# The mixer's inverse root-mean-squares: spread by TensorE from a repeated column instead of from VectorE's diagonal matrix

## What is computed

```python
y = (y_fw + y_bw) + xs * (xs @ fcD_w.T + D)        # "in" and "fd"
yz = y * silu(z)
y = yz * rsqrt(mean(square(yz), -1) + 1e-05) * norm_w   # "out": mean of squares; "scale"
h = y @ out_w.T
...
h = xmid + alpha * xmid + (1 - alpha) * h          # after the second turn
x = x_init + h @ w_up.T + b_up                     # "up", "rest"
```

## Time and profile before

| | before |
|---|---|
| time, median of 3 runs | 755.34 us (755.06 to 757.87) |
| span of the profiled execution | 756.9 us |
| PE busy | 713.5 us (94%) |
| DVE, ACT, POOL busy | 474.8, 318.3, 314.5 us (63%, 42%, 42%) |
| chain that ended last, by engine | PE 76%, DVE 12%, issue 5%, ACT 2%, POOL 1% |
| the mixer in the span | about 487 to 556 us |

### The profile page before, as it was taken

One profiled execution on the slowest core, in us unless ns is written; L12 is line 12 of the kernel. 1 busy time (PEld: TensorE's weight loads), 2 busy tenths in 40 slices (PEclk: granted clock), 3 DMA queues, 4 the chain that ended last, 5 costly groups with the idle time before them and its releaser, 6 DMA issues.

```text
span 756.9 us, 10266 instructions
## 1 busy us (share of the span) xinstructions
PE 713.5 (94%) x3718; PEld 431.1 (57%) x3718; DVE 474.8 (63%) x716; ACT 318.3 (42%) x536; POOL 314.5 (42%) x254
## 2 busy tenths in 40 slices
PE   4998899999999999889999999999789999999998
PEld 2444334333333332258788888554358788877886
DVE  3787677888888885237765558768895433338211
ACT  3311267677767767751335310554234223223100
POOL 0325673756565574861456233115431222125300
PEclk9999799999999999999999999999889999999999
DMA  8357516263251200230023100213010111111111
GB/s 307 107 126 220 124 43 164 73 123 54 72 123 26 30 3 29 75 113 14 29 62 105 56 1 0 78 50 66 1 68 1 57 55 39 44 55 57 42 69 42
DMA packets 24111, 53.00 MB, mean 70 GB/s; under 512 B 4252, under 2 KB 8100, under 8 KB 23044
## 3 DMA queue, kind: packets, MB, share of 16 engines
q1 hardware_dynamic: 24068, 52.44, 25.0%
HBM read 45.63 MB, written 6.60 MB: 69 GB/s over the span
## 4 chain that ended last, share of the span: by engine, by line
PE 76%; DVE 12%; issue 5%; DMA 2%; ACT 2%; SPq 2%; POOL 1%; DVEq 0%; ACTq 0%; POOLq 0%
PE ps L867 73%; DVE mxp L1810 2%; DMA rq<-in_mask 1%; DVE st L1652 1%; PE ps L884 1%; DVE xnb L1676 1%; ACT pr L1456 1%; DVE x L2007 1%; PE ps L1051 1%; DVE rt L1691 1%; DVE x L1894 1%; PE ps L1119 0%; DVE dg L2041 0%; SPq L717 0%; DVE qsw L1861 0%
## 5 line engine op out<-in xcount | busy, mean ns | idle before, releaser
L867 PE MATMUL ps<-arena 128*128 128x512 f32 (+1 forms) x1404 | 325.9, 392 | 1.4 <-DVE arena L1695 0.7
L867 PEld LDWEIGHTS ps<-arena 128*128 128x128 f32 (+1 forms) x1404 | 259.6, 186 | 59.3 <-DVE arena L1695 1.4
L1810 DVE TENSOR_REDUCE mxp<-ps 128x2 f32<-128x1024 f32 (+3 forms) x160 | 172.8, 1115 | 44.5 <-PE ps L867 43.9
L1456 ACT ACTIVATE pr<-ps 128x512 f32<-128x512 f32 x288 | 162.1, 596 | 75.7 <-PE ps L867 71.9
L867 PE MATMUL ps<-Qst,Kst 99*128 99x512 bf16 x288 | 100.2, 389 | 6.1 <-ACT pr L1456 4.8
L867 PE MATMUL ps<-Kst,Qst 96*128 96x512 bf16 (+3 forms) x384 | 98.6, 334 | 5.4 <-DVE mxp L1810 4.2
L2248 POOL TENSOR_TENSOR pr<-pr,cap 128x512 int32<-128x512 int32 x56 | 71.1, 1285 | 38.3 <-ACT pr L1456 38.3
L867 PE MATMUL ps<-pr,vr 128*32 128x512 f32 x576 | 76.5, 604 | 0.0
L867 PEld LDWEIGHTS ps<-Qst,Kst 99*128 99x128 bf16 x288 | 24.5, 98 | 79.7 <-ACT pr L1456 63.9
L867 PEld LDWEIGHTS ps<-Kst,Qst 96*128 96x128 bf16 x384 | 36.4, 99 | 51.3 <-DVE mxp L1810 20.2
L2347 POOL TENSOR_TENSOR arena<-raw,arena 128x1024 fp32r<-128x1024 f32 x11 | 26.7, 2431 | 80.2 <-ACT arena L1530 80.2
(11 more groups left out here) (203 smaller groups left out, 822.2 us busy)
## 6 DMA issues: line engine op xcount, KB each, us to landing
wmr<-in_wmr SPq DMA_DIRECT2D x8, 1280.0 KB, 11.0
raw<-in_w SPq DMA_DIRECT2D x16, 512.0 KB, 3.3
Qst<-q_parts SPq DMA_DIRECT2D x42, 128.0 KB
q_parts<-qparts SPq DMA_DIRECT2D x3, 768.0 KB, 5.0
x<-in_x SPq DMA_DIRECT2D x8, 256.0 KB, 6.0
wm<-in_wm SPq DMA_DIRECT2D x4, 512.0 KB, 7.5
raw<-in_up SPq DMA_DIRECT2D x8, 256.0 KB, 2.6
raw<-in_down SPq DMA_DIRECT2D x8, 256.0 KB, 2.6
```

What stands on the lines that cost most here:

```text
L867: return nc.tensor.matmul(outp, lhs, rhs, start=start, stop=stop, skip_group_check=True)
L1456: A(pr[:, k % PRING, :], ps[:, 4 + k % 2, :], ACT.Exp, scale=float(DH) ** -0.5).then_inc(exp_done, 1)
L1810: V.tensor_reduce(mxp[:, kh, g0:g0 + heads, i].rearrange("p (b e) -> p b e", e=per), units, AXX, ALU.max)\
```

## The change

`dg`, its four VectorE instructions and its semaphore go. In the step `scale` TensorE now issues four multiplications of 128 x 128: the stationary operand is one column of `hrs`, read 128 times with a stride of zero, the moving one the identity. Element (i, j) of the product is the sum over k of hrs[k] times identity[k, j], that is hrs[j] on every row. TensorE waits for `hrs` itself (`mr_ready`). GpSimd, before it overwrites `hrs`, now waits until the last `rbc` is written instead of for `dg`, and its `shift` no longer waits for `dg`. Apart from the removals VectorE's list has one move: `rest` of the second half comes behind `fd` and `scale` of the second turn.

```diff
-MIXER_DVE = [("fd", 0, 0), ("rows", 0, 0), ("dg", 0, 0), ("scale", 0, 0), ("fd", 0, 1), ("centred", 0, 0),
-             ("centred", 0, 1), ("dg", 0, 1), ("fd_first", 1, 0), ("scale", 0, 1), ("fd_second", 1, 0), ("rest", 0, 0), ("merge", 0, 0),
-             ("rest", 0, 1), ("dg", 1, 0), ("fd", 1, 1), ("scale", 1, 0), ("dg", 1, 1), ("up", 0, 0), ("scale", 1, 1),
+MIXER_DVE = [("fd", 0, 0), ("rows", 0, 0), ("scale", 0, 0), ("fd", 0, 1), ("centred", 0, 0),
+             ("centred", 0, 1), ("fd_first", 1, 0), ("scale", 0, 1), ("fd_second", 1, 0), ("rest", 0, 0), ("merge", 0, 0),
+             ("fd", 1, 1), ("scale", 1, 0), ("rest", 0, 1), ("up", 0, 0), ("scale", 1, 1),
              ("up", 0, 1), ("up", 1, 0), ("up", 1, 1)]
...
                 elif kind == "scale":
 
-                    pe.wait_ge(dg_ready, 2 * y + hf + 1)
+                    pe.wait_ge(mr_ready, 2 * y + hf + 1)
                     b = bank_of(pe, ("rbc", y, hf))
-                    mm(ps[:, b, :], ones[:, :], dg[:, :, :].rearrange("p t n -> p (t n)"), True, True)\
-                        .then_inc(full_b[b], 1)
+                    for t in range(4):
+                        last = mm(ps[:, b, tl(t)], hrs[:, t:t + 1].to_broadcast([P, P]), ident[:, :], True, True)
+                    last.then_inc(full_b[b], 1)
...
-                elif kind == "dg":
-                    dve.wait_ge(mr_ready, 2 * y + hf + 1)
-                    if 2 * y + hf:
-                        filled(dve, ("rbc", y if hf else 0, 1 - hf))
-                    V.tensor_tensor(dg[:, :, :], ident[:, :].unsqueeze(1).to_broadcast([P, 4, P]),
-                                    hrs[:, :].unsqueeze(2).to_broadcast([P, 4, P]), ALU.mult).then_inc(dg_ready, 1)
...
                 if kind == "out":
                     pool.wait_ge(ms_ready, 2 * y + hf + 1)
                     if 2 * y + hf:
-                        pool.wait_ge(dg_ready, 2 * y + hf)
+                        filled(pool, ("rbc", y if hf else 0, 1 - hf))
                     nc.gpsimd.tensor_tensor(hrs[:, :], hms[:, :], mh[:, :], ALU.pow).then_inc(mr_ready, 1)
                 elif kind == "shift":
-                    pool.wait_ge(dg_ready, 2)
                     for t in range(4 * hf, 4 * hf + 4):
                         rest(t)
```

More of the change, by code:

```diff
@@ L491, in adaln_two_blocks @@
         yz = at("yz", [P, 2, T], F32, ACT_B + 80 * 1024)
-        dg = at("dg", [P, 4, P], F32, HT_B + 26 * 1024)
         rb = at("rb", [P, HALF], F32, HT_B + 28 * 1024)
@@ L607, in adaln_two_blocks @@
         eps_ready, hor_ready = sem("eps_ready"), sem("hydra_out_copied")
-        ms_ready, mr_ready, dg_ready = sem("mean_squares_ready"), sem("inverse_rms_ready"), sem("inverse_rms_diagonal_ready")
+        ms_ready, mr_ready = sem("mean_squares_ready"), sem("inverse_rms_ready")
         mixw_in = sem("mixer_weights_loaded")
```

## The result

| | before | with the change |
|---|---|---|
| time, median of 10 runs | 757.85 us (755.06 to 758.74) | 752.39 us (750.0 to 755.11) |
| ratio to before | 1 | 0.9938 (95%: 0.9925 to 0.9952) |
| span of the profiled execution | 756.9 us | 752.4 us |
| PE busy | 713.5 us | 709.7 us |

The change makes the kernel 0.62% faster, 4.7 us (0.0062 of 757.85; by the interval 3.6 to 5.7). The median of before rose from the three runs shown ahead of the prediction to 757.85 with seven more; the ratio is taken in the same rounds. A time is 1.8 us more than the span of the same execution, as in the changed kernel's profiled one (754.24 and 752.4) and in every other run whose span is listed.

What follows compares the result with a forecast made beforehand. PE was busy 94% of the span, so only VectorE work that TensorE waits for counted. VectorE's add at 552.03 coming 4.7 us sooner, taken from the 755.34 us median, gave 750.6 us, range 747.6 to 753.5.

Steps and rivals of the forecast that it cites:

- the forecast's own case: Mixer, second turn: VectorE's instruction with `midf` waits out GpSimd's second product; 4.7 us sooner, 749.6 to 751.6 us, chance 0.42.
- the rival of loads in series: TensorE's weight loads and passes go one after the other, 1.78 us for each `rbc`; 752.0 us, chance 0.13.
- TensorE's own work: In `scale`, eight passes with weight loads at 0.123 us each: 0.98 us, 0.1 more for each `rbc`.
- GpSimd's shifts: First turn: shifts start at about 519.8 instead of 520.54; VectorE's first `rest` ends at 532.0 to 532.6, from 532.02.
- VectorE, second turn: With `rest` and `dg` no longer ahead, `fd` (1,1) starts at 534.4 to 535.0 instead of 537.60.
- S: The moment TensorE begins `up` (0,0) in the second turn; forecast at 540.6, 3.3 us sooner than 543.88.
- The fourth `rbc` and the race: Fourth `rbc` no longer waits; VectorE's `midf` instruction comes 0.1 us after GpSimd's second product; next add 4.7 us sooner.
- the first rival: VectorE's instruction with `midf` comes ahead of GpSimd's second product; 6.8 us sooner, 748.5 us, chance 0.28.
- Remain in kind, up to 0.3 us longer: Behind the mixer: the idle 2.62 us before the transposes and their slow pace stay, up to 0.3 us longer.
- The rival of a clock that falls in the new gaps: TensorE's granted clock falls in the second turn's new short waits; only 3.4 us sooner, 752 us, chance 0.07.

Runs made afterwards that it cites:

- e4: The changed kernel with each of TensorE's 16 products of 128 x 128 issued twice, result unchanged; ratio to the kernel before 0.9935.
- e8: The changed kernel with each of TensorE's 16 products of 128 x 128 issued twice, timed once more; ratio to the kernel before 0.9969.
- e1: The kernel before with only the move of the second half's `rest` behind `fd` and `scale`, diagonal kept; ratio to the kernel before 0.9942.
- e2: The changed kernel with `rest` put back ahead of `fd`, so only the diagonal's removal remains; ratio to the kernel before 0.9994.
- e7: The changed kernel once more, without any edit; ratio to the kernel before 0.9946.
- e5: The changed kernel with three overwritten 128 x 512 TensorE products filling idle time before the last layer norm's first transposes; ratio to the kernel before 0.9952.
- e3: The changed kernel with GpSimd's second product of weight low parts waiting until VectorE has written the last half of `hof`; ratio to the kernel before 0.9888.
- e10: The changed kernel with GpSimd's second product of weight low parts delayed until the last `hof`, timed again; ratio to the kernel before 0.9923.

## Why the prediction was right, point by point

**The size.** 4.7 us were forecast and 4.7 measured by the ratio; the median of 752.39 lies 1.8 above the forecast 750.6 (outside the 749.6 to 751.6 of the forecast's own case, inside the range), since the median of before rose by 2.5. By that median alone the rival of loads in series (752.0 us) would have looked right; the trace decides against it (0.89 us for an `rbc`, not 1.78). Within the mixer it was 4.98. The match of the span (752.2 forecast, 752.4 measured) is partly luck: 1.05 us of chance ahead of the mixer and 1.56 us lost in B nearly cancel.

**TensorE's own work.** Of the bounds 0.107 to 0.22 us for a pass with its load I took 0.123, and it is 0.111. An `rbc` costs 0.89 us, so the 0.1 us more in each did not come. Loads of 0.19 us each are hidden behind passes 0.111 us apart, although all use the whole array, so the rule of the Trainium skill that was weighed (TensorE: Matmul & The Clock Gate, "The mechanism") does not hold for this stream; e4 and e8 show what it would have cost. A stride of zero in the stationary operand costs nothing: its loads take 0.186 to 0.192 us, as those of the mixer's other float32 products do (0.190 to 0.192 on average).

**GpSimd's shifts.** They started 0.8 us sooner against the start of A and the first `rest` ended 0.37 us later (531.34 - 493.84 = 37.50; 532.02 - 494.89 = 37.13 before); 0 to 0.6 was forecast.

**VectorE, second turn.** `fd` starts at 533.66, 39.82 us into A where it was 42.71: 2.9 us sooner (2.6 to 3.2 forecast). S is 3.46 us sooner (3.3 forecast). e1 and e2 confirm that this is the move's work. Of the 3.46 us, 0.57 are the clock that no longer falls there. The sum has that in it without naming it: it prices `out` and the squares behind `yz` at full speed (0.86 + 1.71), where the rows of before hold 3.29 us.

**The fourth `rbc` and the race.** L2049 was issued at S + 3.92 (3.9 forecast) and GpSimd's first product at S + 1.50 (1.49). GpSimd's second product began 0.11 us before L2049 (POOL alone, around 545 us):

```profile
543.18 2.34 POOL L2341 TENSOR_TENSOR arena<-raw,arena 128x1024 fp32r<-128x1024 f32 x1
```

So L2049 lost the race by the 0.1 us that were forecast. It waited 2 us, and the next add came at S + 6.63 (6.75). One small term was off: `rbc` began at S + 1.80, not at S + 1.72, since its first load waited for `hrs`. That cost nothing, for `hof` was held by VectorE's own add and statistics until S + 3.21 (3.2 forecast). L2049 lost in all three traces with this mixer, each time by 0.10 to 0.11 us (it lasted 2.78, 2.79 and 2.78 us in the change, e7 and e5), so the first rival, 748.5 us, did not turn on chance in what was traced. e3 is that rival made true: A is 7.04 us shorter than before (6.8 forecast), and the medians are 749.55 us and, in e10, 750.66.

**What hung behind it.** "Remain in kind, up to 0.3 us longer" is the one step that failed in size, by 1.3 us in this trace: the slow clock did not stay at the first transposes but came at the second, where it costs. In the second trace of the changed kernel it was 0.3 us. The rival of a clock that falls in the new gaps, of 0.23 and 0.27 us, did not happen; the window of the changed kernel from 536 to 546 us has it at 1.00:

```profile
536.00:546.00 10.00, 7.67 (x36) 4.49 (x34) 9.85 (x13) 1.58 (x3) 5.64 (x3) 1.00 0.17 60
```

## What to carry to other kernels

Before you move work off an engine, ask what stands ahead of the late instruction on its list: here moving four instructions that nobody waited for was worth 3.35 us of the mixer, and the diagonal's removal by itself 1.1. An instruction of VectorE with two inputs in SBUF was longer by nearly a whole instruction of GpSimd (2.78 instead of 0.75 us beside one of 2.35), so a removed one can hand that wait to the next such instruction. Delaying GpSimd's work took the wait away; giving the waiting instruction an input in PSUM might too, as the adds beside GpSimd in rows 3 suggest, but was not tried. When runs scatter by 0.5%, take a stretch between two events that all traces share: this one repeated within 0.02 us where the clock stayed at 1.00, and tells edits of 1 us apart. Look at its granted clock first.

## What was not expected of the hardware

How long VectorE waits for GpSimd depends on where its instruction falls beside GpSimd's. With the shifts 0.8 us sooner, a product of `yz` in the first turn became 1.67 us long, from 1.13 before and 0.69 alone, with nothing lost since TensorE was not waiting for it:

```profile
518.69 12.10 POOL L2336 TENSOR_TENSOR x<-x,Bbc 128x512 f32<-128x512 f32 x8
...
520.06 1.67 DVE L2032 TENSOR_TENSOR yz<-yz,sz 128x512 f32<-128x512 f32 x1
```

And the place at which TensorE's granted clock falls decides its price: 3.45 instead of 1.97 us for 16 transposes cost nothing, and a fall that came some 8 us after their start cost 1.56 us.
